# Neighbour attention: the normalisation one step later, DVE's order across two steps, the mask product ahead of the wait for the differences

## The chip, the cores and the metric

The kernel runs on one core of a Trainium2 chip. The metric is the device time of one execution in microseconds; the median of several runs is given. The engines are TensorE (PE, with its weight loads PEld), VectorE (DVE), ScalarE (ACT), GpSimd (POOL) and SyncE (SP, which here only issues transfers). Each works through its own list of instructions in order; semaphores tie the lists together.

## The reference

A small model of two layers: neighbour attention, self attention, a low-rank feed-forward, a second layer with cross attention, a state-space convolution and a binary feed-forward. The change concerns only the neighbour attention of the first layer, which takes features (8 batches, 32 channels, 512 points) and runs twice:

```python
for inds in inds_list:                      # 4 orders of the points, windows of k = 10
    neigh = gather(feats, inds)
    gf = jnp.concatenate([jnp.broadcast_to(center, (B, N, k, C)), neigh - center], axis=-1)
...
scores = jnp.einsum('bihd,bjhd->bhij', qh, qh) / np.float32(np.sqrt(headdim))
attn = jax.nn.softmax(scores, axis=-1)
out = jnp.einsum('bhij,bjhd->bihd', attn, qh).reshape(B * N, k, total)
fused = out @ W_lin.T + b_lin
...
g1 = _get_graph_features(f0, inds_list, perm1, W_lin1, b_lin1)
h1 = jnp.einsum('oc,bnkc->bonk', W_conv1, g1)
h1 = _lrelu(_instance_norm(h1, (2, 3)))
feats1 = h1.max(axis=-1)
```

So every point has a 10 x 10 softmax in each head over its window of neighbours, then a weighted sum, a linear map, a norm over all points and a maximum over the 10 places. The second run takes `feats1` and gives 64 channels instead of 32.

## The kernel before, in words

`phase_window_attention` (L834) does this, once for stage 0 (32 output channels, G = 1 group of rows in PSUM) and once for stage 1 (64 channels, G = 2). A stage works in TB = 44 steps: two halves of the batches, and for each SBS = 22 steps over the points, 24 points a step (the last step of a half has 12). For step g:

- POOL, `windows_minus_centre`: the differences of every window to its centre (L925). The first step of a half adds ten small subtractions at the border (L936, L937).
- PE, `scores`: a product that writes the mask into PSUM (L974), then 32 small products of differences with the masked features hi and lo (L982).
- DVE: `top_of`, the maximum of each window (L1079); `shift`, scores less maximum (L1086). ACT: `exponent` (L1039). DVE: `sums` (L1097) and `inverse`, the reciprocal (L1104).
- POOL, `normalise`: exponential times reciprocal (L946).
- PE, `turn`: four transposes (L994). ACT, `bring`: their evacuation (L1046). PE, `weigh`: the own-value product (L1010) and the products with the values (L1021 in stage 0, L1026 in stage 1).
- DVE, `take`: every second step, one statistics (L1115) and one maximum (L1116) for each of the G groups.

In the first half ACT also prepares the second half's hi and lo, one instruction every second step (`second_half`, L1055 and L1059). SP loads the values of four steps at once into one of two buffers (L906, L911), as soon as the last weighted sum that used the buffer is made.

What orders the work is written by hand. `ticks` (L879) goes over t; each entry is a lag and a body, and the body is called for g = t - lag, so one tick of an engine works on several steps. Nothing is reordered later. The scores, the transposed weights, the normalised weights, the maxima, sums and reciprocals have two buffers each, the exponentials three; each body waits for the semaphore of what it reads and of what last used its buffer.

Of the kernel before, what the change touches and what calls it, by code (L numbers as in the profile page):

```python
# [827 lines left out]
VRING = 2  # L828
GROUP = 2
GROUPS = -(-SBS // GROUP)  # L830
SCORE_LAG, SUM_LAG, TURN_LAG = 1, 2, 3


def phase_window_attention(nc, T, D, W, O, name):  # L834
# [8 lines left out]
    def blocks_of(g):  # L843
        return min(PAIRBLK, BLOCKS - g % SBS * PAIRBLK)

    with Scope(nc, name) as s:
# [32 lines left out]
        def ticks(*turns):  # L879

            for t in range(TB + TURN_LAG + 1):
                for lag, body in turns:
                    if 0 <= t - lag < TB:
                        body(t - lag)

        with nc.Block() as block:
# [29 lines left out]
            def _(pool):  # L916
# [41 lines left out]
                    if g:  # L958
                        windows_minus_centre(g)

                ticks((0, later_windows), (SUM_LAG, normalise))

            @block.tensor
            def _(pe):
                def scores(g):
                    q, k, u = g // SBS, g % SBS, g % 2
                    if k == 0:
                        pe.wait_ge(high_ready, q + 1)
                        pe.wait_ge(low_ready, q + 1)
                    pe.wait_ge(diff_ready, g + 1)  # L970
                    if g >= 2:
                        pe.wait_ge(sub_done, g - 1)
                    n = blocks_of(g)
                    nc.tensor.matmul(scoreP[u][:, 0:n].rearrange("p k r x -> p (k r x)"), T["rowsof"][:],  # L974
                                     T["mask" if k else "mask0"][:, 0:n * HC * SPAN], start=True, stop=False, skip_group_check=True)
                    for blk in range(n):
                        for r in range(QB):
                            for part, last in ((hi, False), (lo, True)):
                                for b in range(SUBS):
                                    sub = blk * BLK + b * SUB  # L980
                                    at = k * SB + sub
                                    mm = nc.tensor.matmul(scoreP[u][b * STEP:b * STEP + SROWS, blk, r],  # L982
                                                          diff[u][:, r, sub:sub + SUB].rearrange("p n i -> p (n i)"),
                                                          part[q][:, r, :, at:at + SPAN],
                                                          start=False, stop=last, skip_group_check=True)
                    mm.then_inc(score_ready, 1)
# [11 lines left out]
                def weigh(g):  # L998
# [29 lines left out]
                    mm.then_inc(out_ready, 1)  # L1028

                ticks((TURN_LAG, turn), (SCORE_LAG, scores), (TURN_LAG, weigh))  # L1030

            @block.scalar
# [38 lines left out]
            def _(dve):  # L1071
# [50 lines left out]
                for h in range(HEADS):  # L1122
                    ins = vec.tensor_scalar(lo[0][:, :, h, :], W["lo"][:, 0:QB, :], T["headmask"][:, h:h + 1], None, ALU.mult)
                ins.then_inc(low_ready, 1)
                ticks((SUM_LAG, sums), (SCORE_LAG, top_of), (SUM_LAG, inverse), (SCORE_LAG, shift), (TURN_LAG + 1, take))
                dve.wait_ge(taken, HALVES * GROUPS)
                tail = s.sem("tail")
                go = Steps(dve, tail)
# [1136 lines left out]
```

## Time and profile before

| | |
|---|---|
| median of 3 runs | 1376.63 us (1371.64 to 1384.47) |
| the profiled execution | 1368.01 us, span 1366.3 us |
| its TensorE clock, mean | 0.857 of full speed |
| PE, DVE, ACT, POOL busy | 74%, 56%, 32%, 32% of the span |
| POOL L946 waits for DVE L1104 | 99.4 us, 86 of 88 times |
| PE L994 waits for POOL L946 | 93.3 us |
| DVE L1079 waits for PE L982 | 76.7 us, 71 times |

The span is that of the whole program; stage 0 of the neighbour attention lies at about 244 to 429 us of it, stage 1 at 521 to 729 us. A row of the timeline gives the start, the duration, the engine, the line, the operation with output and inputs, and in brackets how long the engine idled before it and what ended that. PEclk is the granted clock of TensorE as a share of 2.4 GHz: 0.50 is 1.2 GHz.

### The profile page before, as it was taken

How to read it: one execution, taken by the hardware profiler on the slowest of the kernel's cores; microseconds unless marked ns; L12 is line 12 of the kernel's file. 1: busy time of each engine (PE TensorE's matmuls, PEld its weight loads, DVE VectorE, ACT ScalarE, POOL GpSimd, SP SyncE). 2: the span in 40 equal slices, each digit the busy share in tenths (PEclk: the TensorE clock that was granted, in tenths of full speed). 3: DMA queues.
4: the chain of work that ended last, by engine and by line, in shares of the span. 5: the costliest groups of instructions: out<-in, count | busy, mean ns of one | idle time of the engine just before them, and what ended most of it. 6: DMA issues, size and time to landing. Idle time of an engine off the chain costs nothing. (4 is left out here: it accounts for less than half of the span.)

```text
span 1366.3 us, 28657 instructions
## 1 busy us (share of the span) xinstructions
PE 1014.2 (74%) x10354; PEld 751.7 (55%) x10354; DVE 768.7 (56%) x1848; ACT 442.1 (32%) x893; POOL 443.7 (32%) x366
## 2 busy tenths in 40 slices
PE   3772479366664893777673899994997799998698
PEld 2551249244543482555451799994743567775475
DVE  4869873476776844776775323236342356564542
ACT  0499511254333122452220122224001255663100
POOL 3000235777773467676750200000000054430000
PEclk9995596698897996885875899997997799998799
DMA  3851301222223033322310454540553435451000
GB/s 112 295 203 56 80 1 66 55 37 35 42 38 69 15 124 102 78 56 69 73 44 8 128 152 143 156 140 23 172 147 101 169 111 183 177 192 21 10 0 16
DMA packets 183727, 126.40 MB, mean 93 GB/s; under 512 B 99637, under 2 KB 157813, under 8 KB 182606
## 3 DMA queue, kind: packets, MB, share of 16 engines
q1 hardware_dynamic: 183082, 120.82, 30.1%
q10 hardware_dynamic: 548, 4.25, 0.8%
q8 instruction: 65, 1.06, 0.3%
q14 instruction: 32, 0.26, 0.1%
HBM read 110.27 MB, written 14.76 MB: 92 GB/s over the span
## 5 line engine op out<-in xcount | busy, mean ns | idle before, releaser
L925 POOL TENSOR_TENSOR attend_diff<-win_ext,win_F 128x960 f16<-128x960 f32 x88 | 163.2, 1855 | 0.0
L994 PE MATMUL attend_prob_t<-core_ident,attend_pnorm 124*128 124x124 f32 x344 | 65.4, 320 | 93.4 <-POOL attend_pnorm L946 93.3
L946 POOL TENSOR_TENSOR attend_pnorm<-attend_prob,attend_inv 124x480 f32<-124x480 f32 x88 | 86.7, 985 | 99.4 <-DVE attend_inv L1104 99.4
L1039 ACT ACTIVATE attend_prob<-attend_centred 124x480 f32<-124x480 f32 x88 | 52.2, 594 | 167.7 <-DVE attend_centred L1086 167.7
L1079 DVE TENSOR_REDUCE attend_top<-attend_score 124x32 f32<-124x480 f32 x88 | 56.6, 644 | 76.9 <-PE attend_score L982 76.7
L994 PEld LDWEIGHTS attend_prob_t<-core_ident,attend_pnorm 124*128 124x128 f32 x344 | 41.4, 159 | 105.9 <-POOL attend_pnorm L946 105.5
L360 ACT ACTIVATE sort_signs<-sort_keysB,sort_key 128x512 bf16 x128 | 90.5, 739 | 13.0 <-DMA sort_keysB<-scratch_keys 13.0
L610 PE MATMUL order_ordered<-order_place,order_own 128*32 128x512 bf16 x768 | 69.0, 401 | 23.3 <-POOL order_own L563 23.3
L1288 DVE TENSOR_SCALAR attn_qT<-proj_qp,attn_bq,attn_gq 128x256 f32 x32 | 17.4, 543 | 122.3 <-ACT attn_sq L1267 122.3
L593 DVE TENSOR_SCALAR order_place<-core_iota,points_rank 128x512 bf16<-128x512 f16 x256 | 73.6, 365 | 16.2 <-PE order_ordered L610 13.6
L1809 DVE TENSOR_REDUCE cross_negtop<-cross_score 128x1 f32<-128x512 f32 x64 | 44.2, 691 | 59.8 <-PE cross_score L1680 59.8
L1680 PE MATMUL cross_score<-cross_kT,cross_qblock 128*128 128x512 f32 x128 | 71.7, 644 | 5.7 <-ACT cross_prob L1745 3.0
L982 PEld LDWEIGHTS attend_score<-attend_hi,attend_diff 128*60 128x60 f16 x1376 | 55.6, 123 | 33.2 <-issue 33.2
L1097 DVE TENSOR_REDUCE attend_total<-attend_prob 124x32 f32<-124x480 f32 x88 | 56.0, 636 | 30.1 <-ACT attend_prob L1039 30.0
L1046 ACT COPY attend_probT<-attend_prob_t 128x496 f32<-128x496 f32 x88 | 49.2, 559 | 65.2 <-PE attend_prob_t L994 65.2
L1597 POOL TENSOR_TENSOR cross_raw<-cross_raw,binary_base 128x2688 f32<-128x2688 f32 x8 | 47.0, 5872 | 70.1 <-DMA cross_raw<-in_fw_dram 70.1
L610 PEld LDWEIGHTS order_ordered<-order_place,order_own 128*32 128x32 bf16 x768 | 41.0, 99 | 50.8 <-DVE order_place L593 27.4
L982 PE MATMUL attend_score<-attend_hi,attend_diff 128*60 128x60 f16 x1376 | 66.0, 210 | 0.0
L974 PE MATMUL attend_score<-core_mask,core_rowsof 128*128 128x480 bf16 x88 | 38.3, 435 | 35.5 <-POOL attend_diff L937 28.2
L1240 PE MATMUL proj_qp<-core_xnT,attn_wq 128*128 128x256 f32 x256 | 63.3, 391 | 1.4 <-DMA attn_wv<-in_Wv_dram 1.4
L982 PE MATMUL attend_score<-attend_lo,attend_diff 128*60 128x60 f16 x1376 | 64.2, 207 | 0.0
L1373 POOL COPY attn_attT<-att_flipped 32x512 f32<-32x512 f32 x4 | 2.4, 602 | 187.7 <-DVE att_flipped L1359 187.7
(323 smaller groups left out, 2467.6 us busy)
## 6 DMA issues: line engine op xcount, KB each, us to landing
binary_base<-in_fmean_dram SPq DMA_DIRECT2D x8, 1344.0 KB, 8.0
cross_raw<-in_fw_dram SPq DMA_DIRECT2D x8, 1344.0 KB, 11.0
attend_vT<-scratch_values SPq DMA_DIRECT2D x160, 60.0 KB
sort_ctxT<-in_ctxT_dram SPq DMA_DIRECT2D x8, 1024.0 KB, 6.1
attn_wq<-in_Wq_dram SPq DMA_DIRECT2D x32, 256.0 KB
attn_wk<-in_Wk_dram SPq DMA_DIRECT2D x32, 256.0 KB
attn_wv<-in_Wv_dram SPq DMA_DIRECT2D x32, 256.0 KB
att_wo<-in_Wo_dram SPq DMA_DIRECT2D x32, 256.0 KB, 2.6
```

Source lines behind the costliest of these rows:

```text
L360: nc.scalar.activation(signs[t][:], keysB[:, bass.ds(b * N + at * N, N)], ACT.Sign, scale=-1.0, bias=key[:].bitcast(F32)[:, bass.ds(b * KC ...
L593: vec.tensor_scalar(place[i % RING][:], W["iota"][:], T["rank"][:, bass.ds((b * KC) + (m * B * KC + t), 1)], None, ALU.is_equal).then_inc( ...
L610: mm = nc.tensor.matmul(ordered[u][m * C:(m + 1) * C, :], own[u][:, k, t, :], place[i % RING][:], start=(t == 0 and k == 0), stop=(t == KC ...
L925: ins = nc.gpsimd.tensor_tensor(diff[u][:, :, 0:size], spread, f.unsqueeze(3).to_broadcast([P, QB, size, WIN]), ALU.subtract)
L946: nc.gpsimd.tensor_tensor(pnorm[g % 2][:, 0:n, 0:K].rearrange("p r (h w) -> p r h w", w=SPAN), prob[g % 3][:, 0:n * HEADS].rearrange("p (r ...
L982: mm = nc.tensor.matmul(scoreP[u][b * STEP:b * STEP + SROWS, blk, r], diff[u][:, r, sub:sub + SUB].rearrange("p n i -> p (n i)"), part[q][ ...
L994: mm = nc.tensor.transpose(probP[u][:, x, :], pnorm[u][:, 2 * x:2 * x + 2].rearrange("p r w -> p (r w)"), T["ident"][0:MROWS, 0:MROWS])
L1039: nc.scalar.activation(prob[g % 3][:, 0:n], centred[g % 2][:, 0:n], ACT.Exp, scale=INV).then_inc(exp_done, 1)
L1079: vec.tensor_reduce(top[g % 2][:, 0:blocks_of(g) * HC], seen(g), AX.X, ALU.max).then_inc(top_done, 1)
L1097: vec.tensor_reduce(total[g % 2][:, 0:n], prob[g % 3][:, 0:n], AX.X, ALU.add).then_inc(sum_done, 1)
L1240: mm = nc.tensor.matmul(out[u][:], w[u][:, c, :], T["xnT"][:, c, :], start=(c == 0), stop=(c == KC - 1))
L1680: nc.tensor.matmul(scoreP[g % 2][:], qblock[u][:, g].rearrange("p r q -> p (r q)"), kT[u][:], start=True, stop=True).then_inc(score_made, 1)
```

## The change

`NORM_LAG` is new and stands at 3: the normalisation is called for g = t - 3 and no longer for t - 2. `TURN_LAG` goes from 3 to 4, and with it the transposes, their evacuation, the weighted sums and `second_half`; `take` goes from t - 4 to t - 5. On DVE the four bodies of a tick change their order. In `scores` the wait for the differences stands behind the mask product. Buffers, instructions and transfers stay the same in number and shape.

```diff
--- before.py
+++ after.py
@@ -828,7 +828,7 @@
 VRING = 2
 GROUP = 2
 GROUPS = -(-SBS // GROUP)
-SCORE_LAG, SUM_LAG, TURN_LAG = 1, 2, 3
+SCORE_LAG, SUM_LAG, NORM_LAG, TURN_LAG = 1, 2, 3, 4
 
 
 def phase_window_attention(nc, T, D, W, O, name):
@@ -958,7 +958,7 @@
                     if g:
                         windows_minus_centre(g)
 
-                ticks((0, later_windows), (SUM_LAG, normalise))
+                ticks((0, later_windows), (NORM_LAG, normalise))
 
             @block.tensor
             def _(pe):
@@ -967,12 +967,12 @@
                     if k == 0:
                         pe.wait_ge(high_ready, q + 1)
                         pe.wait_ge(low_ready, q + 1)
-                    pe.wait_ge(diff_ready, g + 1)
                     if g >= 2:
                         pe.wait_ge(sub_done, g - 1)
                     n = blocks_of(g)
                     nc.tensor.matmul(scoreP[u][:, 0:n].rearrange("p k r x -> p (k r x)"), T["rowsof"][:],
                                      T["mask" if k else "mask0"][:, 0:n * HC * SPAN], start=True, stop=False, skip_group_check=True)
+                    pe.wait_ge(diff_ready, g + 1)
                     for blk in range(n):
                         for r in range(QB):
                             for part, last in ((hi, False), (lo, True)):
@@ -1122,7 +1122,7 @@
                 for h in range(HEADS):
                     ins = vec.tensor_scalar(lo[0][:, :, h, :], W["lo"][:, 0:QB, :], T["headmask"][:, h:h + 1], None, ALU.mult)
                 ins.then_inc(low_ready, 1)
-                ticks((SUM_LAG, sums), (SCORE_LAG, top_of), (SUM_LAG, inverse), (SCORE_LAG, shift), (TURN_LAG + 1, take))
+                ticks((SCORE_LAG, top_of), (SUM_LAG, sums), (SCORE_LAG, shift), (SUM_LAG, inverse), (TURN_LAG + 1, take))
                 dve.wait_ge(taken, HALVES * GROUPS)
                 tail = s.sem("tail")
                 go = Steps(dve, tail)
```

On DVE, in the steady part of stage 0, one step with its take, before (`top` are the maxima, `centred` scores less maxima, `total` the sums, `inv` the reciprocals; `exp`, `score`, `sum`, `norm`, `outr` are the semaphores of exponentials, scores, sums, normalisation and weighted sums):

```order
L1097 TENSOR_REDUCE attend_total<-attend_prob 124x32 [waits attend0_exp]
L1079 TENSOR_REDUCE attend_top<-attend_score 124x32 [waits attend0_score]
L1104 RECIPROCAL attend_inv<-attend_total 124x32 [waits attend0_norm,attend0_sum]
L1086 TENSOR_TENSOR attend_centred<-attend_score,attend_top 124x480 [waits attend0_exp,attend0_top]
L1115 BN_STATS attend_stats<-attend_outp 128x6 [waits attend0_outr]
L1116 TENSOR_REDUCE points_f<-attend_outp 128x48
```

and now:

```order
L1079 TENSOR_REDUCE attend_top<-attend_score 124x32 [waits attend0_score]
L1097 TENSOR_REDUCE attend_total<-attend_prob 124x32 [waits attend0_exp]
L1086 TENSOR_TENSOR attend_centred<-attend_score,attend_top 124x480 [waits attend0_exp,attend0_top]
L1104 RECIPROCAL attend_inv<-attend_total 124x32 [waits attend0_norm,attend0_sum]
L1115 BN_STATS attend_stats<-attend_outp 128x6 [waits attend0_outr]
L1116 TENSOR_REDUCE points_f<-attend_outp 128x48
```

Before, a step runs sums, maximum, reciprocal, subtraction; now it runs maximum, sums, subtraction, reciprocal. Maximum and subtraction belong to the step that is one younger than that of sums and reciprocal, in both.

On PE, around the first transposes of stage 0 (`prob_t`) and the mask product behind them; where rows are left out the score products stand. Before:

```order
L994 MATMUL attend_prob_t<-core_ident,attend_pnorm 128x124 [waits attend0_norm]
L994 MATMUL attend_prob_t<-core_ident,attend_pnorm 128x124 x3
L974 MATMUL attend_score<-core_mask,core_rowsof 128x480 [waits attend0_sub,attend0_diff]
...
L1010 MATMUL attend_outp<-attend_ownhot,attend_own 128x240 [waits attend0_valuesin0,attend0_hotin]
L1021 MATMUL attend_outp<-attend_probT,attend_vT 64x60 [waits attend0_copied]
```

and now:

```order
L994 MATMUL attend_prob_t<-core_ident,attend_pnorm 128x124 [waits attend0_norm]
L994 MATMUL attend_prob_t<-core_ident,attend_pnorm 128x124 x3
L973 MATMUL attend_score<-core_mask,core_rowsof 128x480 [waits attend0_sub]
...
L1010 MATMUL attend_outp<-attend_ownhot,attend_own 128x240 [waits attend0_valuesin0,attend0_hotin]
L1021 MATMUL attend_outp<-attend_probT,attend_vT 64x60 [waits attend0_copied]
```

The mask product (L974 before, L973 now) has lost its wait for the differences, `diff`; the scores behind the transposes of step 0 are those of step 3 and no longer those of step 2.

On POOL, at the start of stage 0, before:

```order
L955 MEMSET attend_vT 128x2048 x2
L925 TENSOR_TENSOR attend_diff<-win_ext,win_F 128x960
L925 TENSOR_TENSOR attend_diff<-win_ext,win_F 128x960 [waits attend0_score]
L946 TENSOR_TENSOR attend_pnorm<-attend_prob,attend_inv 124x8x60 [waits attend0_inv]
L925 TENSOR_TENSOR attend_diff<-win_ext,win_F 128x960 [waits attend0_score]
```

and now:

```order
L955 MEMSET attend_vT 128x2048 x2
L925 TENSOR_TENSOR attend_diff<-win_ext,win_F 128x960
L925 TENSOR_TENSOR attend_diff<-win_ext,win_F 128x960 [waits attend0_score] x2
L946 TENSOR_TENSOR attend_pnorm<-attend_prob,attend_inv 124x8x60 [waits attend0_inv]
L925 TENSOR_TENSOR attend_diff<-win_ext,win_F 128x960 [waits attend0_score]
```

Behind the buffers' clearing, the differences of steps 1, 2 and 3 stand ahead of the first normalisation, where those of steps 1 and 2 stood.

## Rows read from the trace of the kernel before

**Rows 1.** Busy by stretch: us, busy of each engine (instructions), PEclk, DMA share, GB/s.
```profile
256.00:424.00 168.00, 107.21 (x2291) 78.25 (x2291) 114.50 (x222) 66.83 (x97) 123.45 (x98) 0.91 0.23 38
533.00:721.00 188.00, 132.28 (x3023) 93.26 (x3023) 136.49 (x265) 66.46 (x97) 122.95 (x97) 0.76 0.28 67
270.00:330.00 60.00, 39.24 (x885) 28.51 (x885) 43.43 (x84) 34.26 (x42) 47.48 (x34) 0.98 0.23 38
640.00:659.00 19.00, 16.67 (x304) 11.64 (x296) 13.03 (x25) 4.99 (x9) 12.04 (x9) 0.50 0.23 53
```

**Rows 2.** Waits, 250 to 422 us (stage 0): who for whom, total us, times, longest.
```profile
POOL attend_pnorm L946 <- DVE attend_inv L1104: 40.1, 43, 2.6
```

**Rows 3.** Waits, 520 to 720 us (stage 1).
```profile
POOL attend_pnorm L946 <- DVE attend_inv L1104: 59.3, 43, 2.9
```

**Rows 4.** Timeline, one step of stage 0 at 2.4 GHz: start, us, engine, line, operation.
```profile
362.02 1.00 POOL L946 TENSOR_TENSOR attend_pnorm<-attend_prob,attend_inv 124x480 f32<-124x480 f32 x1 [0.71 <-DVE attend_inv L1104]
...
362.99 1.88 POOL L925 TENSOR_TENSOR attend_diff<-win_ext,win_F 128x960 f16<-128x960 f32 x1
...
363.08 0.65 PE L994 MATMUL attend_prob_t<-core_ident,attend_pnorm 124*128 124x124 f32 x4 [1.27 <-POOL attend_pnorm L946]
...
363.76 0.58 ACT L1046 COPY attend_probT<-attend_prob_t 128x496 f32<-128x496 f32 x1 [0.67 <-PE attend_prob_t L994]
...
363.86 0.22 PE L982 MATMUL attend_score<-attend_hi,attend_diff 128*60 128x60 f16 x2
...
364.58 0.66 DVE L1079 TENSOR_REDUCE attend_top<-attend_score 124x32 f32<-124x480 f32 x1 [0.80 <-PE attend_score L982]
...
364.67 0.68 PE L1021 MATMUL attend_outp<-attend_probT,attend_vT 128*64 128x60 f32 x16
...
365.15 0.34 DVE L1104 RECIPROCAL attend_inv<-attend_total 124x32 f32<-124x32 f32 x1
...
365.41 0.59 DVE L1086 TENSOR_TENSOR attend_centred<-attend_score,attend_top 124x480 f32<-124x480 f32 x1
...
365.57 1.00 POOL L946 TENSOR_TENSOR attend_pnorm<-attend_prob,attend_inv 124x480 f32<-124x480 f32 x1 [0.71 <-DVE attend_inv L1104]
...
365.92 0.65 DVE L1115 BATCH_NORM_STATS2 attend_stats<-attend_outp 128x6 f32<-128x480 f32 x1
...
366.04 0.60 ACT L1039 ACTIVATE attend_prob<-attend_centred 124x480 f32<-124x480 f32 x1 [1.69 <-DVE attend_centred L1086]
...
366.49 0.64 DVE L1116 TENSOR_REDUCE points_f<-attend_outp 128x48 f32<-128x480 f32 x1
...
367.05 0.64 DVE L1097 TENSOR_REDUCE attend_total<-attend_prob 124x32 f32<-124x480 f32 x1
```

**Rows 5.** Timeline, one step of stage 1 at 1.2 GHz.
```profile
587.76 1.00 POOL L946 TENSOR_TENSOR attend_pnorm<-attend_prob,attend_inv 124x480 f32<-124x480 f32 x1 [1.31 <-DVE attend_inv L1104]
...
588.82 1.09 PE L994 MATMUL attend_prob_t<-core_ident,attend_pnorm 124*128 124x124 f32 x4 [0.57 <-POOL attend_pnorm L946]
...
590.24 0.26 PE L982 MATMUL attend_score<-attend_hi,attend_diff 128*60 128x60 f16 x2
...
591.74 1.13 PE L1026 MATMUL attend_outp<-attend_probT,attend_vT 64*64 64x60 f32 x32
...
592.34 1.00 POOL L946 TENSOR_TENSOR attend_pnorm<-attend_prob,attend_inv 124x480 f32<-124x480 f32 x1 [1.74 <-DVE attend_inv L1104]
```

**Rows 6.** Timeline of ScalarE, stage 0, first half.
```profile
275.31 2.04 ACT L1055 ACTIVATE attend_hi<-win_ext,core_headmask 128x2112 f16<-128x2112 f32 x1
277.26 0.55 ACT L1046 COPY attend_probT<-attend_prob_t 128x496 f32<-128x496 f32 x1
```

**Rows 7.** SP's issues of the values, and the product that uses them (minimum/median/maximum ns).
```profile
262.19 1.23 SPq L911 DMA_DIRECT2D attend_own<-scratch_own  x3
...
665.31 9.40 SPq L906 DMA_DIRECT2D attend_vT<-scratch_values  x16
...
L1010 PE MATMUL attend_outp<-attend_ownhot,attend_own x132: 218/277/408, 265.9 to 717.6; 72*128 72x240 bf16 x126, 72*128 72x120 bf16 x6
```


## The prediction

> **What bounds the kernel now.** The change touches one function, the neighbour attention, which runs twice: stage 0 (about 244 to 429 us of the span) and stage 1 (521 to 729 us). I read the busy time by stretch first. POOL is busy 123 of 168 us and 123 of 188 us in the two loops, DVE 114 and 136, PE 107 and 132: no engine is full, so something goes round in a circle [rows 1]. The waits say which: POOL's normalisation waits for DVE's reciprocal 43 times, 40.1 us in stage 0 and 59.3 us in stage 1 [rows 2, 3].
>
> The timeline of one step shows the circle [rows 4]. The normalisation starts at 362.02. PE's transpose of it starts 1.06 later (363.08); behind it in PE's order stand the score products of a step two further on (363.86), and DVE can take their maximum only at 364.58, 1.50 after the transpose. The reciprocal that the next normalisation needs stands behind that maximum in DVE's order: 365.15, 0.57 later. Normalisation again at 365.57, 0.42 later. 1.06 + 1.50 + 0.57 + 0.42 = 3.55 us, the whole step. The reciprocal's sums were ready long before; it is only queued. In this step POOL idles 0.71 us, so its own work is 3.55 - 0.71 = 2.84 us.
>
> Stage 1 has two output groups (G = 2), so every second step DVE also runs two pairs of statistics and maximum, one pair being 365.92 to 367.05 = 1.13. Such a step is DVE's own work end to end: 0.57 (maximum) + 0.26 (reciprocal) + 0.51 (subtraction) + 2.26 + 0.57 (sums) = 4.17, and POOL's idle time grows from 0.71 to 1.31 [rows 4, 5]. Stage 1 so alternates 3.55 and 4.15, mean 3.85.
>
> TensorE's clock is a second limit. In stage 0 it is granted at 0.91 of full speed on average, in stage 1 at 0.76 [rows 1]: 18% and 48% of the time at 1.2 GHz instead of 2.4. A step at 1.2 GHz takes 592.34 - 587.76 = 4.58 us [rows 5]. That is 30 and 90 us at the low clock; without the fill and the halves' boundary (some 8 and 10 us, where POOL's small subtractions set the pace whatever the clock) it is some 5 slow steps in stage 0 and 17 or 18 in stage 1. They cost 5 x 1.02 + 17.5 x 0.72 = 17.7 us against an all-fast loop.
>
> **The change, part by part.** *One step later.* Normalisation of step g now stands after the differences of g + 3 on POOL, transpose and weighted sum beside the scores of g + 3 on PE. The circle is now: normalisation g, transpose g, scores g + 3, maximum g + 3, and then, by DVE's new order, sums g + 2, subtraction g + 3, reciprocal g + 2, normalisation g + 2. It spans two steps instead of one. Its length from the same rows: 1.06 + 1.50 + 0.57 (maximum) + 0.57 (sums, a reduction of the same shape) + 0.51 (subtraction) + 0.42 = 4.63, so 2.32 us a step [rows 4]. It no longer binds.
>
> What is late next, at 2.4 GHz: POOL's 2.84; DVE's 0.57 + 0.57 + 0.51 + 0.26 = 1.91 plus one pair in two steps in stage 0 (2.48) and two pairs in two steps in stage 1 (1.91 + 1.13 = 3.04); PE from transpose to the end of the weighted sum 364.67 + 0.68 - 363.08 = 2.27. So 2.84 a step in stage 0, set by POOL, and 3.04 in stage 1, set by DVE.
>
> *The second half's operands.* In each first half ScalarE builds the second half's masked operands, one 2.04 us instruction every second step, right behind the exponential and ahead of the next evacuation of the transpose [rows 6]. That makes a circle over two steps: exponential 0.51, the instruction 1.95, evacuation 0.60, weighted sum 0.60, then PE's next transpose and scores 1.50, maximum and sums 1.14, subtraction to exponential 0.63: 6.93 us, 3.47 a step [rows 4, 6]. Before, with the reciprocal's 0.26 in place of the sums' 0.57, it was 6.6, hidden under 2 x 3.55. Now it binds for about 12 steps a stage.
>
> *The order on DVE* alone (sums between maximum and subtraction) would lengthen the path; with the lag it costs nothing, because sums find their exponential done: subtraction to exponential 0.63 plus exponential 0.64 = 1.27, while subtraction, reciprocal and the next maximum already fill 1.34 [rows 4].
>
> *The mask product ahead of the wait for the differences:* nothing. On POOL the differences of g come before the normalisation that PE's preceding transpose waits for, so that wait is always already met. Cover gone, it would save at most the 0.37 us product in the first steps of a half.
>
> *Fill and drain:* the first normalisation has one more difference (1.88 less the wait it replaces) ahead of it: 1.5 us a stage, 3 in all, lost.
>
> **The sum.** A stage has 44 steps, 43 intervals: one at the halves' boundary, some 6 us and POOL's, three in the drain, 39 regular, of which 12 with the second-half operands.
> Stage 0: 27 x (3.55 - 2.84) + 12 x (3.55 - 3.48) = 19.2 + 0.8 = 20.0.
> Stage 1: 27 x (3.85 - 3.04) + 12 x (3.85 - 3.48) = 21.9 + 4.4 = 26.3.
> Less the fill: 46.3 - 3 = 43.3 us, for loops at 2.4 GHz before and after.
> Clock: a slow step becomes PE's own work, 588.82 to 591.74 + 1.13 = 4.05 us [rows 5], so it is still shorter than 4.58, but costs 1.21 (stage 0) or 1.01 (stage 1) against a fast one. How many there will be, the trace of before can't show. Bounds: none, and all. Nearest rows: 2.27 us of PE work in 3.55 kept 2.4 GHz for 60 us in stage 0 (clock 0.98), while stage 1's alternating steps kept losing it [rows 1]. The new fast steps hold PE's 2.27 in about 3, denser than either. So I keep the 5 slow steps around fill and boundary and half of stage 1's: 5 x 1.21 + 9 x 1.01 = 15.1 in place of 17.7, 2.6 gained.
> Total 43.3 + 2.6 = 46 us. The profiled execution took 1368.0 (span 1366.3): 1322. The median shown is 1376.6, 8.6 above it; the same 46 off that is **1331**, my forecast for the median.
>
> One rule bears on the clock. In 640 to 659 us PE was busy 16.67 of 19 us and stayed at 0.50 throughout [rows 1], so busy time alone did not lift the clock here. The Trainium skill (TensorE: Matmul & The Clock Gate, Part 1: The HAM clock gate) has it that the throttled state is the default and activity releases it. Taken plainly, that would hold the denser loop at 2.4 GHz throughout and give the first rival's time; the 19 us stretch speaks against so plain a reading.
>
> **The rivals.**
> 1. *The clock never falls* in the loops. For: the new step is denser than the 60 us that held. Against: fill and boundary keep their gaps. 43.3 + 17.7 = 61 us gained: 1316.
> 2. *Slow for half the steps.* For: stage 1's 48%. 39 x 1.11 = 43.3 lost of 61, 18 gained: 1359.
> 3. *The values arrive late.* The values of four steps are loaded together, into the buffer whose last weighted sum has just ended, and are wanted by the product five steps on: room for 5 steps less the 0.9 us of that sum and what stands ahead of it on PE. The longest issue was 9.40 plus 1.23, and the first part's last piece was used at 265.9, 2.5 us after its issue ended (263.4) [rows 7]: 13.1 us. Room was 16.8, and is now 13.3 (stage 0) or 14.3. It fits barely. If loads stretched to 16 us, steps become 16.9 / 5 = 3.38: 27 x 0.54 + 27 x 0.34 = 24 lost: 1355.
> 4. *The other side: PE stays at 1.2 GHz throughout.* The step would be 4.05 everywhere: 39 x 0.50 + 39 x 0.20 = 27.3 more than the fast loops before, less the 17.7 already paid, plus 3 fill and some 4 for drains run slowly: 17 us, 1393, slower by 1.2%. It decides once 61 / 1.11 = 55 of the 78 steps are slow. For: 640 to 659. Against: the 60 us at 0.98.
> 5. *The lag doesn't open the circle* (some buffer's wait still ties normalisation g + 1 to scores g + 3). Then the new DVE order lengthens a one-step circle to 4.63, over 80 us slower: 1457. Reciprocal g + 2 waits for normalisation g, normalisation g for transpose g - 2: both well inside two steps, so hardly.
> 6. *An unseen wait keeps 3.55*: 1377.
>
> **How the numbers follow.** Forecast 0.72, rival 1 0.10, rival 2 0.08, rival 3 0.04, rival 4 0.02, rival 5 0.01, rival 6 0.03. Each of the first four is over 1% faster; about 1% is what a measurement can tell from no change. Of the 0.94 I move 0.01 to "same" for a gain between rivals 2 and 6: faster 0.93, same 0.04, slower 0.03. Range: from below rival 1 (1310, the baseline's own runs spread by some 6 either way) to just short of rivals 2 and 3 (1352), which leaves them and 4 to 6 out.
>
> **What would show it.** POOL's normalisations 2.84 apart in stage 0's second half, with almost no wait for the reciprocal; 3.48 in pairs in the first half; about 3.04 in stage 1's second half with DVE without gaps; slow steps at 4.05. POOL's total wait for the reciprocal falls from 99 us to under 50. Wrong if the intervals stay at 3.55 (the circle), if granted clock falls under 0.7 in both stages (rivals 2, 4), or if the own-value product waits for its DMA every fourth step (rival 3).

## The result, and the profile after

Median 1317.95 us (4 runs, 1314.59 to 1324.07), against 1376.32 us of the kernel before in the same comparison (4 runs). The ratio, which compares runs in the faster of the kernels' two states alone, is 0.9636, interval 0.9595 to 0.9678, a gain of 3.6%; the two medians as they stand would give 0.958. The forecast was 1331, its range 1310 to 1352. The profiled execution took 1314.59 us (span 1312.9), 53.4 us less than the one before.

Where these 53.4 us lie, by the places of the same instructions in both traces (a stage runs from its first clearing on POOL to the end of DVE's last instruction, L1137; the differences are those of the unrounded times):

| stretch | before | after | difference | predicted |
|---|---|---|---|---|
| stage 0 | 184.1 | 167.6 | -16.6 | -17.5 |
| stage 1 | 208.1 | 175.5 | -32.6 | -28.3 |
| everything else | 974.1 | 969.9 | -4.2 | 0 |

The stretches by engine, after (stretch, its us, busy us of PE, PEld, DVE, ACT and POOL with instruction counts, granted clock, DMA share, GB/s):

```profile
256.00:404.00 148.00, 111.62 (x2290) 82.33 (x2290) 109.57 (x218) 63.24 (x96) 121.16 (x97) 0.86 0.26 43
510.00:680.00 170.00, 116.12 (x3055) 83.35 (x3055) 141.31 (x284) 64.28 (x98) 126.58 (x100) 0.85 0.32 76
275.00:325.00 50.00, 36.82 (x756) 27.47 (x756) 32.98 (x66) 26.77 (x34) 37.28 (x28) 0.86 0.23 38
360.00:394.00 34.00, 28.68 (x666) 20.91 (x662) 30.88 (x63) 12.78 (x24) 34.00 (x25) 1.00 0.31 51
632.00:660.00 28.00, 22.08 (x658) 15.84 (x657) 28.00 (x57) 9.48 (x18) 23.36 (x19) 1.00 0.36 84
```

The first two rows answer to the first two of [rows 1]: nearly the same instructions in 148 us for 168, and in 170 for 188. The last two are the steady stretches of the second halves, where each stage has an engine that is full: POOL 34.00 of 34 us in stage 0, DVE 28.00 of 28 us in stage 1. No engine was full anywhere in [rows 1]. The third row is stage 0's first half: there none is, POOL is busy 37 of 50 us.

Waits after, stage 0 (who for whom, total us, times, longest):

```profile
PE attend_outp L1021 <- ACT attend_probT L1046: 25.5, 22, 2.5
...
POOL attend_diff L925 <- PE attend_score L982: 13.9, 12, 2.7
POOL attend_pnorm L946 <- DVE attend_inv L1104: 9.3, 22, 1.9
...
PE attend_outp L1010 <- DMA attend_own<-scratch_own: 3.2, 2, 2.7
```

and stage 1:

```profile
PE attend_outp L1026 <- ACT attend_probT L1046: 28.4, 22, 2.3
...
POOL attend_pnorm L946 <- DVE attend_inv L1104: 21.1, 24, 3.1
...
POOL attend_diff L925 <- PE attend_score L982: 6.3, 6, 2.3
...
PE attend_outp L1010 <- DMA attend_own<-scratch_own: 4.1, 2, 3.5
```

Against [rows 2, 3] POOL's wait for the reciprocal fell from 40.1 to 9.3 us and from 59.3 to 21.1 us. Three waits are new or larger. POOL now waits for the scores (20.2 us; the differences' buffer is not yet free). The own-value product waits for its DMA (7.3 us in the two stages, 3.1 before). And PE's weighted sum waits for the evacuation, where before it did so little:

```profile
PE attend_outp L1021 <- ACT attend_probT L1046: 6.9, 9, 0.8
...
PE attend_outp L1026 <- ACT attend_probT L1046: 4.9, 8, 0.7
```

One step of stage 0 after (timeline: start, us, engine, line, operation, idle before it and its releaser), the counterpart of [rows 4]:

```profile
367.29 1.00 POOL L946 TENSOR_TENSOR attend_pnorm<-attend_prob,attend_inv 124x480 f32<-124x480 f32 x1
...
368.25 1.88 POOL L925 TENSOR_TENSOR attend_diff<-win_ext,win_F 128x960 f16<-128x960 f32 x1
...
368.35 0.64 PE L994 MATMUL attend_prob_t<-core_ident,attend_pnorm 124*128 124x124 f32 x4 [0.49 <-POOL attend_pnorm L946]
...
368.96 0.34 DVE L1104 RECIPROCAL attend_inv<-attend_total 124x32 f32<-124x32 f32 x1
...
369.85 0.66 DVE L1079 TENSOR_REDUCE attend_top<-attend_score 124x32 f32<-124x480 f32 x1 [0.55 <-PE attend_score L982]
...
370.10 1.00 POOL L946 TENSOR_TENSOR attend_pnorm<-attend_prob,attend_inv 124x480 f32<-124x480 f32 x1
...
370.42 0.64 DVE L1097 TENSOR_REDUCE attend_total<-attend_prob 124x32 f32<-124x480 f32 x1
...
370.98 0.65 DVE L1086 TENSOR_TENSOR attend_centred<-attend_score,attend_top 124x480 f32<-124x480 f32 x1
...
371.55 0.34 DVE L1104 RECIPROCAL attend_inv<-attend_total 124x32 f32<-124x32 f32 x1
...
372.89 1.01 POOL L946 TENSOR_TENSOR attend_pnorm<-attend_prob,attend_inv 124x480 f32<-124x480 f32 x1
```

Follow the circle: normalisation 367.29, transpose 368.35, maximum 369.85, sums 370.42, subtraction 370.98, reciprocal 371.55. With the 0.42 us to a normalisation that is 4.68 us (forecast: 4.63), but the normalisation it serves is the one after the next, 5.60 us on, at 372.89. The one at 370.10 took the reciprocal of 368.96, 1.14 us old. POOL shows no idle time; its pitch is 2.80 us.

In stage 1 the same engine, second half:

```profile
632.58 1.01 POOL L946 TENSOR_TENSOR attend_pnorm<-attend_prob,attend_inv 124x480 f32<-124x480 f32 x1
...
635.81 1.00 POOL L946 TENSOR_TENSOR attend_pnorm<-attend_prob,attend_inv 124x480 f32<-124x480 f32 x1 [0.39 <-DVE attend_inv L1104]
...
638.62 1.00 POOL L946 TENSOR_TENSOR attend_pnorm<-attend_prob,attend_inv 124x480 f32<-124x480 f32 x1
```

2.80 and 3.23 take turns, 6.03 for two steps or 3.02 a step: every second time POOL waits 0.39 us for a DVE that has no gap.

The time between the starts of POOL's 44 normalisations, added up over the first 18 intervals (the first half), the next 7 (the half's last step, the boundary, the refilling) and the last 18, with the us of it that TensorE was granted 1.2 GHz:

| | first 18 | next 7 | last 18 | at 1.2 GHz |
|---|---|---|---|---|
| before, stage 0 | 66.7 | 30.9 | 61.2 | 25.8 |
| after, stage 0 | 64.7 | 27.7 | 48.2 | 38.4 |
| before, stage 1 | 74.8 | 32.2 | 70.9 | 80.6 |
| after, stage 1 | 64.3 | 26.3 | 54.6 | 31.7 |

Stage 0's first half gained 2 us of 67; its second half 13 of 61. Two things hold the first half back. One is the clock: 21.2 us of these 18 intervals ran at 1.2 GHz, 8.8 before. The other is the second-half operands' circle, as the next rows show (ScalarE, stage 0, first half):

```profile
287.36 0.60 ACT L1039 ACTIVATE attend_prob<-attend_centred 124x480 f32<-124x480 f32 x1 [2.64 <-DVE attend_centred L1086]
287.87 2.04 ACT L1055 ACTIVATE attend_hi<-win_ext,core_headmask 128x2112 f16<-128x2112 f32 x1
289.81 0.55 ACT L1046 COPY attend_probT<-attend_prob_t 128x496 f32<-128x496 f32 x1
```

The evacuation follows the 2.04 us instruction without a pause: the transposes had been ready, and PE's weighted sum, which starts at 290.42, had idled 1.34 us for it.

The own-value product behind the halves' boundary, SP's issues and PE:

```profile
335.57 8.22 SPq L906 DMA_DIRECT2D attend_vT<-scratch_values  x16
343.83 1.23 SPq L911 DMA_DIRECT2D attend_own<-scratch_own  x3
...
346.48 0.38 PE L1010 MATMUL attend_outp<-attend_ownhot,attend_own 72*128 72x240 bf16 x1 [2.66 <-DMA attend_own<-scratch_own]
```

The values of the second half's first four steps can be issued only when the weighted sum of step 19 has ended (335.5), and the last part of a half has only two steps; the third step from there wants them. Issues of 8.22 + 1.23 us take longer than three short steps, and PE waits 2.66 us (3.51 in stage 1).

### The profile page after: what moved, and what is told of

Read it like the earlier page. It is cut to its first block and busy times, and to the rows that moved or that the text cites. A ratio compares the mean times of both kernels' runs of the same rounds, so it can differ in the third digit from the quotient of the medians.

```text
span 1312.9 us, 28573 instructions
## 1 busy us (share of the span) xinstructions
PE 1001.5 (76%) x10354; PEld 745.5 (57%) x10354; DVE 762.1 (58%) x1848; ACT 437.4 (33%) x893; POOL 439.9 (34%) x366
## 5 line engine op out<-in xcount | busy, mean ns | idle before, releaser
L925 POOL TENSOR_TENSOR attend_diff<-win_ext,win_F 128x960 f16<-128x960 f32 x88 | 163.3, 1858 | 20.3 <-PE attend_score L982 20.2
L610 PEld LDWEIGHTS order_ordered<-order_place,order_own 128*32 128x32 bf16 x768 | 41.8, 100 | 49.2 <-DVE order_place L593 26.2
L1767 POOL TENSOR_TENSOR cross_qblock<-cross_qT,core_kvmask 128x1024 f32<-128x1024 f32 x8 | 15.2, 1901 | 143.3 <-DVE cross_qT L1782 141.3
L1246 PEld LDWEIGHTS proj_vp<-attn_wv,core_xnT 128*128 128x128 f32 x512 | 62.2, 192 | 1.7
L1246 PE MATMUL proj_vp<-attn_wv,core_xnT 128*128 128x128 f32 x512 | 62.3, 275 | 0.0
L1699 PEld LDWEIGHTS cross_mix<-cross_val,cross_probT 128*128 128x128 f32 x512 | 62.2, 192 | 0.1
L1699 PE MATMUL cross_mix<-cross_val,cross_probT 128*128 128x16 f32 x512 | 61.7, 253 | 0.0
```

Of the source, the lines that this page charges most:

```text
L610: mm = nc.tensor.matmul(ordered[u][m * C:(m + 1) * C, :], own[u][:, k, t, :], place[i % RING][:], start=(t == 0 and k == 0), stop=(t == KC ...
L925: ins = nc.gpsimd.tensor_tensor(diff[u][:, :, 0:size], spread, f.unsqueeze(3).to_broadcast([P, QB, size, WIN]), ALU.subtract)
L1246: mm = nc.tensor.matmul(vP[u][:, t, :], T["xnT"][:, c, t * P:(t + 1) * P], wv[u][:, c, :], start=(c == 0), stop=(c == KC - 1))
L1699: mm = nc.tensor.matmul(mixP[own][:, head, :], probT[g % 2][:, sc * P:(sc + 1) * P], val[own][:, sc, head * XD:(head + 1) * XD], start=(sc ...
```

## The experiments

All were compared with the kernel before on the chip they ran on; a ratio is to that, with its interval.

**1. The lags alone.** The change without its other two parts: DVE's old order, mask product behind the wait.

```diff
-                ticks((SCORE_LAG, top_of), (SUM_LAG, sums), (SCORE_LAG, shift), (SUM_LAG, inverse), (TURN_LAG + 1, take))
+                ticks((SUM_LAG, sums), (SCORE_LAG, top_of), (SUM_LAG, inverse), (SCORE_LAG, shift), (TURN_LAG + 1, take))
```

> The changed kernel with DVE's old order (sums, maximum, reciprocal, subtraction) and the mask product behind its wait again: the lags alone. My theory: the lags open the circle and carry nearly the whole gain; the order on DVE only matters where DVE binds. In the old order the sums stand right behind the subtraction of the step before wherever there is no take, and wait for its exponential: 1.27 us from subtraction to sums, of which the subtraction fills 0.51. So DVE's step without take is 1.91 + 0.76 = 2.67 us, with take 4.17 in stage 1: mean 3.42 there against 3.04, 27 steps, 10 us more; the circle through the second half's operands is 0.3 us shorter for two steps, 12 steps in each stage, 4 us less. Together 6 us slower than the changed kernel: 1324, ratio to before 0.962 to 0.967; POOL's interval in stage 0's second half 2.8 to 2.9, in stage 1's second half 2.7 and 4.15 in turn. Rival: the new DVE order is what lets two steps interleave, the lags alone leave the wait of the reciprocal behind the maximum as it was: intervals stay at 3.55 and the time at 1376.

1315.76 us (6 runs), ratio 0.9605 (0.9559 to 0.9652): what the whole change gives (0.9595 to 0.9678), and a little under the expected ratio (0.962 to 0.967). The 6 us by which it was expected to be slower than the change aren't there. The lag carries the gain. But the parts of the loops differ: 58.0, 28.8, 49.4 in stage 0 and 60.0, 28.0, 60.4 in stage 1. Against the change the first halves are 6.7 and 4.3 us shorter, and stage 1's second half is 5.8 us longer. For the first halves the circle of the second half's operands accounts for some 2 us a stage: it has the reciprocal in it and not the sums, and two steps take 2.79 + 3.85 = 6.64 us, not 6.99, in six turns. The rest is mostly the clock of one execution. Experiment 4 differs from this kernel in DVE's order alone, and its first halves are 60.5 and 61.6 us, only 2.5 and 1.6 longer. DVE in stage 1's second half:

```profile
650.78 0.59 DVE L1086 TENSOR_TENSOR attend_centred<-attend_score,attend_top 124x480 f32<-124x480 f32 x1
652.04 0.65 DVE L1097 TENSOR_REDUCE attend_total<-attend_prob 124x32 f32<-124x480 f32 x1 [0.67 <-ACT attend_prob L1039]
```

In the old order the sums follow directly on the subtraction whose exponential they need, and where no statistics lie between them DVE waits 0.67 us. The clock was lower here too (0.87 over these 18 intervals, 0.97 in the change), so not all of the 5.8 us is this wait.

**2. The order alone**, in the kernel before (the same line of DVE's order, the old lags).

```diff
-                ticks((SUM_LAG, sums), (SCORE_LAG, top_of), (SUM_LAG, inverse), (SCORE_LAG, shift), (TURN_LAG + 1, take))
+                ticks((SCORE_LAG, top_of), (SUM_LAG, sums), (SCORE_LAG, shift), (SUM_LAG, inverse), (TURN_LAG + 1, take))
```

> The kernel before with DVE's new order and nothing else. My theory: the circle still closes in one step and is longer by the sums (0.57) and the subtraction (0.51) that now stand between maximum and reciprocal: 3.55 + 1.08 = 4.63 us at 2.4 GHz, in both stages, 39 steps each: 42 + 30 = 72 us more than fast loops of before, and slow steps cost another 1.0 each, so 1445 to 1500 (ratio 1.05 to 1.09). Rival (the order helps by itself, the reciprocal of an older step interleaves with the younger step): below 1376.

1502.96 us (2 runs), ratio 1.0985 (1.0887 to 1.1082): just past the upper end of what was expected (1500, 1.09). POOL:

```profile
270.74 1.00 POOL L946 TENSOR_TENSOR attend_pnorm<-attend_prob,attend_inv 124x480 f32<-124x480 f32 x1 [2.86 <-DVE attend_inv L1104]
...
276.44 1.01 POOL L946 TENSOR_TENSOR attend_pnorm<-attend_prob,attend_inv 124x480 f32<-124x480 f32 x1 [2.86 <-DVE attend_inv L1104]
...
281.11 1.01 POOL L946 TENSOR_TENSOR attend_pnorm<-attend_prob,attend_inv 124x480 f32<-124x480 f32 x1 [1.83 <-DVE attend_inv L1104]
```

and DVE ahead of the last of these:

```profile
278.99 0.66 DVE L1079 TENSOR_REDUCE attend_top<-attend_score 124x32 f32<-124x480 f32 x1 [2.63 <-PE attend_score L982]
279.56 0.64 DVE L1097 TENSOR_REDUCE attend_total<-attend_prob 124x32 f32<-124x480 f32 x1
280.12 0.65 DVE L1086 TENSOR_TENSOR attend_centred<-attend_score,attend_top 124x480 f32<-124x480 f32 x1
280.69 0.34 DVE L1104 RECIPROCAL attend_inv<-attend_total 124x32 f32<-124x32 f32 x1
```

The one-step circle is 4.67 us (281.11 - 276.44; 4.63 was computed), with 5.70 us where PE runs at 1.2 GHz (276.44 - 270.74). Most steps were of the slow kind: granted clock 0.57 in 256 to 480 us, 0.62 in 560 to 800. So the same order that is neutral behind the longer lag costs 10% without it. This is the one-step circle with the new order that rival 5 describes.

**3 and 4. The mask product**, ahead of the wait in the kernel before, and back behind it in the change.

```diff
-                    pe.wait_ge(diff_ready, g + 1)
                     if g >= 2:
                         pe.wait_ge(sub_done, g - 1)
...
                                      T["mask" if k else "mask0"][:, 0:n * HC * SPAN], start=True, stop=False, skip_group_check=True)
+                    pe.wait_ge(diff_ready, g + 1)
```

> The kernel before with only the wait for the differences moved behind the mask product. My theory: nothing, ratio 0.997 to 1.003, because the transposes that stand ahead of it on PE already wait for a normalisation that POOL does after those differences. Rival: the product fills idle time of PE in every step, up to 0.37 us each, 88 steps: 1344.

> The changed kernel with the wait for the differences ahead of the mask product again. My theory: nothing against the changed kernel, ratio to before 0.960 to 0.968. Rival: with the lags PE waits for differences, so the product's 0.37 us in 88 steps comes back on the path: up to 32 us slower than the changed kernel, 1350.

1368.03 us (12 runs), ratio 0.9994 (0.9958 to 1.0029), and 1318.12 us (6 runs), ratio 0.9611 (0.9555 to 0.9668): nothing that these intervals, some 0.4 and 0.6% either way, could tell from zero. The trace of experiment 4 is also a second sight of the change's loops: first 18, next 7 and last 18 intervals of 60.5, 27.5 and 48.0 us in stage 0 and 61.6, 29.1 and 54.8 in stage 1. The second halves repeat within 0.2 us. The first halves do not (64.7 and 64.3 in the change), and nor does their clock: 9.6 us at 1.2 GHz in stage 0's, where the change has 21.2. Whether the place of the mask product or chance makes that difference, one trace of each can't show.

**5. ScalarE's long instruction ahead of the exponential**, in the change. It then lies between the evacuation and the exponential of a tick, and no longer between the exponential and the next evacuation.

```diff
-                ticks((TURN_LAG, bring), (SCORE_LAG, exponent), (TURN_LAG, second_half))
+                ticks((TURN_LAG, bring), (TURN_LAG, second_half), (SCORE_LAG, exponent))
```

> The changed kernel, where ScalarE makes the second half's operands between the evacuation of the transposes and the exponential, and no longer behind the exponential. My theory: the instruction of 1.95 us then lies in ScalarE's idle time (evacuation done 1.2 us after the transposes start, exponential due at 3.27) and the circle of 6.93 us over two steps is gone: first halves run at 2.84 (stage 0) and 3.04 (stage 1) instead of 3.48, 12 steps each: 7.7 + 5.3 = 13 us less than the changed kernel, ratio to before 0.951 to 0.958. Rival: the mean of 3.48 in the first halves is the slow clock and the operands have nothing to do with it: no difference. Second rival: the exponential comes 1.95 us later instead and sums wait: slower than the changed kernel by 10 us or more.

1294.57 us (6 runs), ratio 0.9480 (0.9438 to 0.9523), 0.3% better than the best of the expectation, and faster than both kernels. ScalarE and the stretch of the first half:

```profile
288.39 0.56 ACT L1046 COPY attend_probT<-attend_prob_t 128x496 f32<-128x496 f32 x1
288.84 2.06 ACT L1059 ACTIVATE attend_lo<-stage_lo,core_headmask 128x2112 f16<-128x2112 f16 x1
290.80 0.59 ACT L1039 ACTIVATE attend_prob<-attend_centred 124x480 f32<-124x480 f32 x1
291.30 0.56 ACT L1046 COPY attend_probT<-attend_prob_t 128x496 f32<-128x496 f32 x1
```

```profile
275.00:311.00 36.00, 30.10 (x703) 21.94 (x702) 32.49 (x65) 25.27 (x34) 36.00 (x26) 1.00 0.31 51
```

POOL is now full in the first half too (36.00 of 36, pitch 2.80) and the clock stays at 2.4 GHz, where it was 0.86 in the change's first half. The first 18 intervals fell from 64.7 to 51.0 us and from 64.3 to 53.4: 24.6 us. Of these the circle accounts for 12 x (3.50 - 2.80) = 8.4 and 12 x (3.50 - 3.02) = 5.8 if 12 steps a stage are in it, as forecast; the eight long instructions start 14 steps apart, from first to last, which makes it 9.8 and 6.7. Against the trace of experiment 4 the same intervals fell by 17.7 us, which is nearly the circle alone. So the circle is shown, and the other 7 to 10 us go with the slow steps of the change's own trace. By the ratios the move is worth 1.6% of the kernel before (21 us) against the change and 1.3% against experiment 4.

**6 and 7. POOL a little longer**, by two small clears per step ahead of the normalisation, in the change and in the kernel before.

```diff
                 def normalise(g):
                     n = blocks_of(g) * QB
+                    nc.gpsimd.memset(spare[:, g % 8], 0.0)
+                    nc.gpsimd.memset(spare[:, (g + 4) % 8], 0.0)
```

> The changed kernel with two clearings of 48 columns of a spare buffer on POOL ahead of every normalisation, together s = 0.2 to 0.3 us by the 0.12 us of a 32-column one. My theory: POOL is the bound of stage 0's second half now, so its intervals grow from 2.80 by all of s, over 27 steps 5 to 8 us; in stage 1 DVE binds with 3.04, so only what goes over 0.24 shows, 0 to 2 us. Together 5 to 10 us slower than the changed kernel. Rival: PE or DVE binds in both stages: no difference.

> The same two clearings in the kernel before. My theory: they lie in the 0.71 us in which POOL waits for the reciprocal in every step, intervals stay at 3.55 and 4.15: ratio to before 0.997 to 1.003, POOL's wait shrinks by s. Rival: POOL is on the circle with all its work: as many us slower as in the changed kernel or more, 88 x s = 18 to 26 us.

The change's stage 0:

```profile
369.87 0.14 POOL L944 MEMSET attend_spare<- 128x48 f32 x1
369.94 0.14 POOL L945 MEMSET attend_spare<- 128x48 f32 x1
370.03 1.00 POOL L949 TENSOR_TENSOR attend_pnorm<-attend_prob,attend_inv 124x480 f32<-124x480 f32 x1
...
372.98 1.01 POOL L949 TENSOR_TENSOR attend_pnorm<-attend_prob,attend_inv 124x480 f32<-124x480 f32 x1
```

Two clears overlap and lengthen POOL's step by less than assumed, 0.15 us. All of it shows: 2.95 for 2.80. In stage 1 the pair of intervals stays at 6.04 (before the clears 6.03). In the kernel before, by its profiled execution (1386.57 us, the longest of its ten), intervals at full clock stayed at 3.55 and 4.15, and POOL's wait for the reciprocal shrank instead, from 40.1 to 34.2 us in stage 0. So POOL binds the second half of the change's stage 0, and nothing of the kernel before. The totals (1320.06 us, ratio 0.9640, and 1370.54 us, ratio 1.0002 with 0.9966 to 1.0038) are too coarse for 0.15 us a step, and the 5 to 10 us that were expected don't show in them; the intervals decide it.

**8. DVE a little longer**, by a second reciprocal per step, in the change.

```diff
                     vec.reciprocal(inv[g % 2][:, 0:n], total[g % 2][:, 0:n]).then_inc(inv_done, 1)
+                    vec.reciprocal(spare[:, g % 8, 0:n], total[g % 2][:, 0:n])
```

> The changed kernel with a second reciprocal of the same sums into a spare buffer behind each reciprocal on DVE: 0.26 us more of DVE's time in every step. My theory: in stage 1's second half DVE binds: pairs of intervals grow from 6.03 to 6.55 (3.04 to 3.30 a step), 27 steps, 7 us; in stage 0 DVE has 2.48 + 0.26 = 2.74, under POOL's 2.80, so nothing; first halves nothing (3.48 by ScalarE's circle). Together 5 to 8 us slower than the changed kernel, all of it in stage 1. Rival: POOL binds both stages: no difference; or DVE binds both: 14 us or more.

```profile
643.91 0.34 DVE L1105 RECIPROCAL attend_inv<-attend_total 124x32 f32<-124x32 f32 x1
644.17 0.29 DVE L1106 RECIPROCAL attend_spare<-attend_total 124x32 f32<-124x32 f32 x1
644.38 0.60 DVE L1117 BATCH_NORM_STATS2 attend_stats<-attend_outp 128x6 f32<-128x480 f32 x1
```

It adds 0.21 us a step (644.17 to 644.38). Stage 0's second half keeps 2.80, stage 1's pairs grow from 6.03 to 6.46, by two of these. DVE binds stage 1's second half. The last 18 intervals there took 57.2 us, 2.6 more than in the change. Total 1322.37 us, ratio 0.9650 (0.9597 to 0.9703), in which the expected 5 to 8 us can't be told either.

**9. A third buffer of values**, on top of experiment 5.

```diff
-VRING = 2
+VRING = 3
```

(with a clearing of the third buffer on DVE ahead of its loop)

> The kernel of the run before with the second half's operands moved, and a third buffer for the values (cleared by DVE at the start of the stage), so that a load starts one part earlier. My theory: in the changed kernel the first weighted sum of the second half waits for its values (2.66 and 3.51 us on the own-value product), because the last part of a half has two steps and not four, so that load has the room of three steps only; the interval of 5.5 us behind the halves' boundary becomes 2.8 to 3.3, and there are fewer slow steps behind it. 4 to 8 us less than with the operands moved alone: ratio to before 0.942 to 0.946, and no wait on the own-value product behind a boundary. Rival: the long interval is the slow clock of the boundary itself and stays: ratio 0.948.

The wait of the own-value product for its DMA in stage 0, in experiment 5:

```profile
PE attend_outp L1010 <- DMA attend_own<-scratch_own: 3.2, 3, 2.7
```

and with the third buffer:

```profile
PE attend_outp L1013 <- DMA attend_own<-scratch_own: 0.2, 1, 0.2
```

In stage 1 this wait fell from 3.3 to 0.3 us. The interval behind the boundary fell from 5.52 to 3.71 us in stage 0. The middle 7 intervals are 1.8 and 1.1 us shorter than in experiment 5. The time, 1294.87 us, ratio 0.9459 (0.9418 to 0.9501), can't be told from that of experiment 5, and the 4 to 8 us that were expected don't show. The wait behind the boundary is real and is this buffer's; what it is worth is under what these runs resolve.

**10. Experiment 5 with DVE's old order.**

```diff
-                ticks((SCORE_LAG, top_of), (SUM_LAG, sums), (SCORE_LAG, shift), (SUM_LAG, inverse), (TURN_LAG + 1, take))
+                ticks((SUM_LAG, sums), (SCORE_LAG, top_of), (SUM_LAG, inverse), (SCORE_LAG, shift), (TURN_LAG + 1, take))
```

> The kernel with the second half's operands moved, and DVE's old order (sums, maximum, reciprocal, subtraction). My theory: with the operands out of the way the order on DVE is worth what I worked out for stage 1: 3.42 instead of 3.04 us a step there, over 39 steps 12 to 15 us, and nothing in stage 0 (2.86 against 2.80, 2 us). Ratio to before 0.956 to 0.960, stage 1's intervals in pairs of 6.8, DVE waiting for the exponential ahead of sums. Rival: the order is worth nothing, as the comparison of the lags alone with the whole change suggests: ratio 0.948.

1305.31 us (6 runs), ratio 0.9549 (0.9513 to 0.9585), where experiment 5 has 0.9480. The sums' wait in stage 1:

```profile
DVE attend_total L1097 <- ACT attend_prob L1039: 14.7, 22, 0.7
```

22 waits of 0.67 us; the pair of steps is 6.80 us and not 6.04, and the 44 normalisations of stage 1 take 146.9 us, not 135.5 (stage 0: 126.5 and 125.5). Stage 0 has the same 22 waits, 14.7 us, and they cost 1 us there, since POOL binds it. So the new order is worth about 10 us once the ScalarE circle is gone. In the change as it was made, experiments 1 and 4 show no gain from it: there it shortens stage 1's second half and lengthens the circle of both first halves.

## Why the prediction was right

**The circle of 3.55 us opens to two steps.** Right. Experiment 1 gets the whole gain from the lag; in the timeline the circle is 4.68 us over two steps (forecast 4.63).

**POOL's 2.84 then sets stage 0, DVE's 3.04 stage 1.** Right: 2.80 and 3.02, each with its engine full, and experiments 6 to 8 lengthen one at a time and find it in its own stage's second half only. POOL's own work was taken as 3.55 less its idle time; that was 0.04 too much.

**The second half's operands, 6.93 us for two steps.** Right: 3.02 + 3.97 = 6.99 in stage 0, 2.86 + 4.14 = 7.00 in stage 1, and with the long instruction elsewhere POOL's 2.80 comes back. Undersized in two ways: it lasts for 14 steps and not 12, and when the clock is at 1.2 GHz a turn of it took 8.4 us (3.02 + 5.42), since PE's part of it is stretched too. The forecast priced a slow step as PE's own work, 4.05.

**The order on DVE at nothing.** Right in the sum (experiment 1), for a reason the text had only half. It compared how long the exponential takes (1.27) with what the new order puts in between (1.34), and saw no wait; it did not ask what the old order would do behind the same lag. The old order's wait stood in the trace of before, in both stages:

```profile
DVE attend_total L1097 <- ACT attend_prob L1039: 15.0, 23, 0.7
```

There it was hidden under the one-step circle. Behind the lag it comes out: 0.67 us in every second step of stage 1, some 5 us over the last 18 intervals. Against that stand the 0.31 us by which sums in place of the reciprocal lengthen the two-step circle of the first halves. That the two cancel is luck of this kernel; experiment 10 has one without the other.

**The mask product at nothing.** Right (experiments 3 and 4).

**Fill, 1.5 us a stage.** From the first clearing to the first normalisation stage 0 took 16.5 us before and 17.7 after: 1.2.

**The clock.** 2.6 us were to be gained, from 5 slow steps staying in stage 0 and 17 or 18 becoming 9 in stage 1. Counting the intervals with a mean granted clock of 0.75 or less, they went from 6 to 9 and from 17 to 9. Stage 1 was as assumed; stage 0 got worse, from 25.8 to 38.4 us at 1.2 GHz, in the first half. PE waits there for the evacuation behind the long instruction, but that doesn't settle the clock: experiment 4 has the same waits (26.0 us, 22 times) and 26.8 us at 1.2 GHz. The price of a slow step was off both ways. The nine low-clock intervals of stage 1 took 32.9 us together, 3.65 each and not 4.05; three of them, at clocks of 0.50 to 0.60, took POOL's 2.79 to 2.90. Against the forecast's fast step they cost 32.9 - 9 x 3.04 = 5.5 us where the sum had 9.1. The nine of stage 0 took 35.4 us and cost 35.4 - 9 x 2.84 = 9.8 where it had 6.1. That the two misses cancel (15.3 against 15.1) is luck. Rival 1, no slow step at all, did not happen, and nor did half the steps run slowly. The Trainium skill (TensorE: Matmul & The Clock Gate, Part 1: The HAM clock gate) holds that activity releases the throttle. The denser loop bears this out in part: the steady stretches held 1.00 with PE busy 28.68 of 34 and 22.08 of 28 us, while [rows 1] show 0.50 with 16.67 of 19.

**Rival 3, values that come late**, was given 0.04 on a room of five steps less 0.9 us. That formula holds inside a half. It is wrong for the first part of the second half, because the part before the boundary has two steps and not four, so the room is three steps: 2.66 and 3.51 us of waiting. PE's waits of this kind add up to 7.3 us in 4 places after, and to 3.1 us in 2 places before. The working had missed this piece, and experiment 9 finds nothing in the total for it.

**The size.** The loops' terms came to 45.8 us (with clock and fill) and the two stages gave 49.2. Stage 0 is 0.9 short: POOL's shorter pitch gives 27 x 0.04 = 1.1 more and the slow steps take 3.7 more; the 1.7 that is left I can't assign. Stage 1 is 4.3 over: 3.6 of it are the cheaper slow steps and 27 x 0.02 = 0.5 DVE's shorter pitch. These are shares of one execution, and which intervals count as slow is a choice (0.75). A further 4.2 us lie in phases whose code is the same, and so are scatter between two executions. The median of before had been shown as 8.6 us above its profiled run, and that of after is 3.4 above its own; the ratio, 0.9636, with the loops' 49.2 us (3.6% of 1368) agrees without it.

## What to carry to other kernels

Count for every circle of waits how many steps it spans, and by what it is closed: here a one-step circle of 3.55 us became one of 4.68 over two, and an order that costs 10% on the first is free on the second. After opening one, write down all circles through the engines that serve in order, the occasional long instruction too: a 2.04 us instruction every second step held the first halves at 3.50 a step, and moving it by one place in its engine's list gave 1.6% of the whole kernel. And compare a new order with the old one *behind the new lag*, not only with the trace of before.

## What the runs showed of the hardware

POOL and DVE ran side by side, one of them full (POOL 34.00 and DVE 30.88 of 34 us in stage 0, DVE 28.00 and POOL 23.36 of 28 in stage 1), and POOL's differences took no longer for it: 1858 ns on average, 1855 before. And where TensorE is in the circle, a longer circle cost twice here: experiment 2's stages ran at clocks of 0.57 and 0.62 with PE busy 141 of 224 and 160 of 240 us, and its circle took 5.70 us at the low clock and 4.67 at full clock.
